# Attention scores as float32 products on two 64-row halves of TensorE, and the softmax by head halves

## What is computed

```
layer 0:  y = layernorm(x) * (1 + gamma1) + beta1
          x = x + attention(y) * tanh(cond @ a1) * 0.1
          z = layernorm(x) * (1 + gamma2) + beta2
          x = x + (gelu(z @ fc1 + b) @ fc2 + b) * tanh(cond @ a2) * 0.1
layer 1:  h = layernorm(x) * (1 + scale) + shift
          q, k = rotary(h @ wq + bq), rotary(h @ wk + bk)
          x = x + softmax(where(mask, q k^T / 4, -inf)) v @ wo + bo
          h = layernorm(x) * (1 + scale) + shift
          x = x + gelu(h @ ff_w1 + b) @ ff_w2 + b
attention: softmax(q k^T / 4) v, per sequence and head, 64 by 64 scores
```

## Time and profile before

| what | value |
|---|---|
| median of 3 runs | 1850.09 us (1849.64 to 1850.42) |
| the profiled execution | 1850.1 us, of which the span of instructions is 1848.3 |
| TensorE matmul busy | 1785.7 us, 97% |
| VectorE busy | 1243.2 us, 67% |
| ScalarE busy | 1229.7 us, 67% |
| GpSimd (POOL) busy | 849.7 us, 46% |
| granted TensorE clock | 0.99 of full on average |
| DMA | 199.84 MB, mean 108 GB/s |
| scores L1077 | 1536 products; mask L1082: 256 |

### The profile page before, as it was taken

How to read it: one execution, slowest core, us unless ns; L and a number is a source line. 1 busy time by engine, 2 the same in 40 slices (tenths; PEclk the granted TensorE clock), 3 DMA queues, 4 the chain that set the end, 5 groups by cost and what they waited for, 6 DMA issues and landing times.

```text
span 1848.3 us, 41687 instructions
## 1 busy us (share of the span) xinstructions
PE 1785.7 (97%) x12623; PEld 1634.5 (88%) x12623; DVE 1243.2 (67%) x2985; ACT 1229.7 (67%) x2265; POOL 849.7 (46%) x1036
## 2 busy tenths in 40 slices
PE   7699999999999999998999999999999999999998
PEld 6688989888989988988889989999999999999986
DVE  6767676667676667676667666776666776666751
ACT  4466766766777766676657766667766667766663
POOL 2233433333433333343635556555566555566544
PEclk8999999999999999999999999999999999999999
DMA  6544435444444435445343333333333333333320
GB/s 165 149 107 126 126 92 123 108 108 127 128 105 105 123 95 133 121 120 120 109 149 104 87 106 93 103 98 108 82 112 93 104 98 108 82 112 92 95 73 34
DMA packets 330275, 199.84 MB, mean 108 GB/s; under 512 B 160994, under 2 KB 314596, under 8 KB 330212
## 3 DMA queue, kind: packets, MB, share of 16 engines
q1 hardware_dynamic: 330212, 199.06, 40.4%
HBM read 80.98 MB, written 17.33 MB: 53 GB/s over the span
## 4 chain that ended last, share of the span: by engine, by line
PE 72%; DVE 11%; issue 7%; ACT 3%; SPq 2%; POOL 2%; DMA 1%; DVEq 0%; POOLq 0%; ACTq 0%
PE C L963 16%; PE D L1154 16%; PE B L963 9%; PE B L1110 8%; PE A L1077 6%; PE B L1096 5%; PE A L963 4%; PE E L963 4%; DVE mx L1429 3%; PE A L1082 1%; DVE o_sb L1453 1%; DVE exps L1435 1%; PE E L1121 1%; PE E L1029 1%; SPq L331 1%
## 5 line engine op out<-in xcount | busy, mean ns | idle before, releaser
L593 POOL TENSOR_TENSOR h_lo<-hact,h_hi 128x512 fp32r<-128x512 f32 x256 | 330.3, 1290 | 251.3 <-ACT h_hi L788 238.5
L1077 PE MATMUL A<-k_pad,q_pad 128*128 128x256 f32 x1536 | 256.7, 294 | 10.3 <-DVE exps L1435 7.1
L1154 PE MATMUL D<-wgt_hi,h_hi 128*128 128x256 f32 x1024 | 263.6, 290 | 0.0
L797 ACT COPY probs_turned<-B 128x512 f32<-128x512 f32 x256 | 149.4, 584 | 169.4 <-PE B L1096 169.2
L1110 PE MATMUL B<-v_blocks,probs_turned 128*128 128x68 f32 x2048 | 254.8, 272 | 1.5 <-ACT probs_turned L797 1.5
L1154 PE MATMUL D<-wgt_lo,h_hi 128*128 128x256 f32 x1024 | 255.7, 282 | 0.0
L1110 PEld LDWEIGHTS B<-v_blocks,probs_turned 128*128 128x128 f32 x2048 | 249.2, 193 | 6.8 <-ACT probs_turned L797 2.6
L783 ACT ACTIVATE hact<-C,b_col 128x512 f32<-128x512 f32 x256 | 175.9, 687 | 83.8 <-PE C L963 81.6
L1077 PEld LDWEIGHTS A<-k_pad,q_pad 128*128 128x128 f32 x1536 | 211.7, 192 | 14.1 <-issue 8.0
L792 ACT ACTIVATE exps<-exps 128x512 f32<-128x512 f32 x256 | 161.4, 632 | 87.4 <-DVE exps L1435 85.3
L1429 DVE TENSOR_REDUCE mx<-A 128x8 f32<-128x512 f32 x256 | 174.2, 681 | 66.1 <-PE A L1082 40.0
(11 more groups left out here) (141 smaller groups left out, 3864.6 us busy)
## 6 DMA issues: line engine op xcount, KB each, us to landing
k_pad<-k_flat SPq DMA_DIRECT2D x512, 64.0 KB, 2.1
q_pad<-q_flat SPq DMA_DIRECT2D x256, 128.0 KB, 2.3
gates<-gates SPq DMA_DIRECT2D x64, 256.0 KB, 4.5
x_bias<-x_bias SPq DMA_DIRECT2D x32, 512.0 KB, 3.5
rotation<-rotation SPq DMA_DIRECT2D x256, 64.0 KB, 1.9
x_in<-in_x SPq DMA_DIRECT2D x16, 512.0 KB, 4.5
gates<-gated_bias SPq DMA_DIRECT2D x32, 256.0 KB, 4.8
x_res<-in_x SPq DMA_DIRECT2D x16, 512.0 KB, 3.9
```

The costliest lines, as they stand in the source:

```text
L593: pool.tensor_tensor(hb[1][:, m % 2, :], hact[:, m % 2, :], hb[0][:, m % 2, :].bitcast(F32), ALU.subtract).then_inc(h_lo, 1)
L1077: ins = nc.tensor.matmul(dst, qpad[g % 2][:, c, p, b, :, :].rearrange("p x s -> p (x s)"), kpad[g % 2][:, c, q, :, b * S:(b + 1) * S], sta ...
L1154: ins = nc.tensor.matmul(Dk[g // 2][:, (g % 2) * D:(g % 2 + 1) * D], hb[p][:, m % 2, g * P:(g + 1) * P], w_slice(q, W_FF2, D, m, 0, D), st ...
```

## The change

Queries and keys stay whole float32 values: q_flat, k_flat, q_pad and k_pad lose the dimension of high and low parts, and `low_qk`, `rotated_low` and the casts of layer 1 fall away. In layer 1 POOL's addition writes the flat buffer itself. `scores` is now called once per group. It makes both sequences' scores as float32 products of 64 rows, 128 weight columns and 128 moving columns: rows 0 to 63 (head half h = 0) into bank A0, rows 64 to 127 (h = 1) into A1, the two halves in turn. In layer 1 two products of 64 rows and 512 columns put the mask row in first, one per bank, with mean_w = 2/128. The second index of all softmax functions is now the head half h instead of the sequence b. The bank of `scores(g)` is free only when `subtract` of both halves of group g-1 is through. TensorE's list: `back(5)` and `hidden(7)` move from the end of a step to behind scores(0) of the next, `back(7)` from behind second_turn(1) to behind scores(1). `scores(3)` moves behind `queries_keys(2)`. ScalarE: `second_norm(3)` now stands ahead of `hidden(7)`, and `second_high(0)` ahead of both exponentials of group 0. VectorE: the first maximum, subtract, maximum, subtract stand together, then z_scale and z_shift. POOL's list is unchanged but for `rotated_low`.

```diff
-        flat = [sb("q_flat", [P, G, KC, 2, P], F32R), sb("k_flat", [P, G, KC, 2, P], F32R)]
-        qpad = [sb(f"q_pad{n}", [P, KC, 2, 2, NX, S], F32R) for n in range(2)]
-        kpad = [sb(f"k_pad{n}", [P, KC, 2, NJ, P], F32R) for n in range(2)]
+        flat = [sb("q_flat", [P, G, KC, P]), sb("k_flat", [P, G, KC, P])]
+        qpad = [sb(f"q_pad{n}", [P, KC, 2, NX, S]) for n in range(2)]
+        kpad = [sb(f"k_pad{n}", [P, KC, 2, P]) for n in range(2)]
...
 # sync
-                    sp.dma_start(kpad[n][r, :, :, j, :].rearrange("p c q n -> p (c q) n").bitcast(F32),
-                                 flat[1][r, g, :, :, :].rearrange("p c q n -> p (c q) n").bitcast(F32))\
-                      .then_inc(spread_in[n], 16)
+                    sp.dma_start(kpad[n][r, :, j % 2, :], flat[1][r, g, :, :]).then_inc(spread_in[n], 16)
...
 # gpsimd, rotated()
-                pool.tensor_tensor(rot_sum[:, i % KC, :], rot_sum[:, i % KC, :], rot_swap[:, i % KC, :], ALU.add)\
-                    .then_inc(rot_added, 1)
+                pool.tensor_tensor(flat[i < KC][:, :, i % KC, :], by_group(rot_sum[:, i % KC, :]),
+                                   by_group(rot_swap[:, i % KC, :]), ALU.add).then_inc(rot_added, 1)
...
 # scalar, step()
+                if c is not None:
+                    second_norm(u - 1, G - 1)
                 if p is not None:
                     hidden(u - 2, p, MC - 1)
                     hidden_high(u - 2, MC - 1)
                 if c is not None:
-                    second_norm(u - 1, G - 1)
+                    second_high(u - 1, 0)
                 if b is not None:
                     exponential(u, 0, 0)
-                if c is not None:
-                    second_high(u - 1, 0)
-                if b is not None:
                     exponential(u, 0, 1)
...
 # tensor
-            def scores(u, layer, g, b, a):
...
+            def scores(u, layer, g, a):
+
+                pe.wait_ge(spread_in[g % 2], upto(u, 2 * NSPREAD, (g // 2 + 1) * NSPREAD))
+                if layer == 1 and g == 0:
+                    pe.wait_ge(mrow_in, upto(u - NT, 16, 16))
+                await_(pe, s_sub, upto(u, 2 * G, 2 * g))
...
+                rows = [slice(64 * h, 64 * h + 64) for h in range(2)]
+                if layer == 1:
+                    for h in range(2):
+                        row = mrow[rows[h], 2 * g * S:2 * (g + 1) * S].rearrange("p (b o s) -> p b o s", b=2, o=1)\
+                            .to_broadcast([64, 2, 4, S])
+                        nc.tensor.matmul(A[h][:, :], mean_w[rows[h], :], row, start=True, stop=False, skip_group_check=True)
+                for b in range(2):
+                    for c in range(KC):
+                        for h in range(2):
+                            n = 2 * b + c
+                            ins = nc.tensor.matmul(A[h][:, n * P:(n + 1) * P],
+                                                   qpad[g % 2][rows[h], c, b, :, :].rearrange("p x s -> p (x s)"),
+                                                   kpad[g % 2][rows[h], c, :, b * S:(b + 1) * S], start=layer == 0,
+                                                   stop=True, skip_group_check=True)
+                            if n == 3:
+                                ins.then_inc(pe_s, 1)
...
 # tensor, step()
                 if b is not None:
-                    scores(u, b, 0, 0, a)
+                    scores(u, b, 0, a)
+                if p is not None:
+                    back(u - 2, MC - 3)
+                    hidden(u - 2, MC - 1)
                 if c is not None:
                     second_turn(u - 1, 0)
-                if b is not None:
-                    scores(u, b, 0, 1, a)
                 if p is not None:
                     back(u - 2, MC - 2)
                 if b is not None:
-                    scores(u, b, 1, 0, a)
+                    scores(u, b, 1, a)
+                if p is not None:
+                    back(u - 2, MC - 1)
+                if b is not None:
                     turn_probs(u, 0, 0, a)
-                    scores(u, b, 1, 1, a)
                     turn_probs(u, 0, 1, a)
...
                 if c is not None:
                     second_turn(u - 1, 1)
-                if p is not None:
-                    back(u - 2, MC - 1)
...
-                    scores(u, b, 3, 0, a)
                 if a is not None:
                     queries_keys(u + 1, a, 2, b)
                 if b is not None:
+                    scores(u, b, 3, a)
                     turn_heads(u, 2, c)
-                    scores(u, b, 3, 1, a)
...
-                if c is not None:
-                    back(u - 1, 5)
-                    hidden(u - 1, 7)
...
 # vector, step()
                     maximum(u, 0, 0)
-                if c is not None:
-                    z_scale(u - 1, 0)
-                if b is not None:
                     subtract(u, 0, 0)
                     maximum(u, 0, 1)
-                if c is not None:
+                    subtract(u, 0, 1)
+                if c is not None:
+                    z_scale(u - 1, 0)
                     z_shift(u - 1, 0)
```

More of the change, by code:

```diff
@@ L679, in step @@
                     hidden_low(u - 1, 4)
-                if a == 1:
-                    rotated_low(u + 1, 2)
-                    rotated_low(u + 1, 3)
                 if n is not None:
@@ L753, in second_high, with lay_flat @@
                 nc.scalar.copy(pair_of(zb[0], pair), E[:, :].rearrange("p (c n) -> p c n", c=KC)).then_inc(z_hi, 1)
-            def high_qk(tile, layer, i):
+            def lay_flat(tile, i):
                 c, keys = i % KC, i < KC
@@ L869, in step @@
                 if a == 0:
-                    high_qk(u + 1, 0, 0)
+                    lay_flat(u + 1, 0)
                 if c is not None:
@@ L877, in step @@
                 if a == 0:
-                    high_qk(u + 1, 0, 1)
+                    lay_flat(u + 1, 1)
                 if b is not None:
@@ L898, in step @@
                 if a == 0:
-                    high_qk(u + 1, 0, 3)
+                    lay_flat(u + 1, 3)
                 if known(u) and u == NT:
@@ L1069, in scores @@
                 if g == 0 and known(u) and u == 0:
-                    pe.wait_ge(*chunk_taken(u, 0, b))
+                    pe.wait_ge(*chunk_taken(u, 0, 1))
                 if g == G - 1 and a is not None:
-                    pe.wait_ge(*chunk_taken(u + 1, a, b))
-                s = slice((2 * g + b) * S, (2 * g + b + 1) * S)
-                for c in range(KC):
-                    dst = A[b][:, c * 256:(c + 1) * 256]
-                    for p, q in BY_WEIGHTS:
-                        ins = nc.tensor.matmul(dst, qpad[g % 2][:, c, p, b, :, :].rearrange("p x s -> p (x s)"),
-                                               kpad[g % 2][:, c, q, :, b * S:(b + 1) * S], start=(p, q) == (0, 0),
-                                               stop=layer == 0 and (p, q) == BY_WEIGHTS[-1])
-                    if layer == 1:
-                        row = mrow[:, s].rearrange("p (o s) -> p o s", o=1).to_broadcast([P, NJ, S])
-                        ins = nc.tensor.matmul(dst, mean_w[:, :], row, start=False, stop=True)
@@ L1086, in turn_probs @@
+            def turn_probs(u, g, h, a):
                 if g == 0:
-                    pe.wait_ge(v_moved, upto(u, 8, 4 * b + 4))
+                    pe.wait_ge(v_moved, upto(u, 8, 4 * h + 4))
                 else:
-                    pe.wait_ge(pv_norm, upto(u, 2 * G, 2 * g + b - 1))
-                if a is not None and g == 2 and b == 1:
+                    pe.wait_ge(pv_norm, upto(u, 2 * G, 2 * g + h - 1))
+                if a is not None and g == 2 and h == 1:
                     pe.wait_ge(y_lo, upto(u + 1, 2, 2))
@@ L1097, in turn_probs, with weigh_values @@
                 ins.then_inc(pe_pt, 1)
-            def weigh_values(u, layer, g, b):
-                if b == 0 and g % 2 == 0:
+            def weigh_values(u, layer, g, h):
+                if h == 0 and g % 2 == 0:
                     pe.wait_ge(v_moved, upto(u, 8, 4 * (g // 2) + 4))
@@ L1624, in step @@
                     subtract(u, 3, 0)
-                if a == 0:
-                    low_qk(u + 1, 2)
                 if a == 1:
@@ L1637, in step @@
                     gate_heads(u, 2)
-                if a == 0:
-                    low_qk(u + 1, 3)
                 if known(u) and u == -1:
```

156 lines of the change are left out of this document (60 added, 96 removed).

## The result

The changed kernel takes **1921.65 us** (1918.64 to 1922.42, median of 4 runs), the kernel before 1850.12 on the same chip (1849.64 to 1850.42, 4 runs): ratio 1.0384, 95% interval 1.0369 to 1.0399. It is 3.8% slower. The forecast was 1914.

The account below looks back on a forecast made before the run. TensorE and VectorE were taken as level in the step's first third, so waits decide. Layer 0 (14 x 2.35 + 2 x 1.1 = 35) and layer 1 (16 x 1.8 = 29) gave +64 on 1850.1: 1914 us, range 1868 to 1975.

Parts of the forecast that it names:

- The price of a block: TensorE's time for one new score block of a group: 1.1 us in layer 0, 1.4 in layer 1.
- (a): From the start of the step (end of project(3)) to second_turn(1): +1.65 us in layer 0, +0.9 in layer 1.
- The exponentials aren't late: ScalarE's exponentials of group 0 were placed as done at about 8.4 and 8.9 us after project(3).
- at the same distance: In layer 1 h_lo(7) was taken to come as long after project(3) as in layer 0, 8.5 us.
- (b): From second_turn(1) to project(0), with VectorE's run deciding: -0.4 us a step in both layers.
- (c): From weigh_values(2,1) to turn_probs(3,0): +1.1 us a step in layer 0, +1.3 in layer 1.
- The sign named for being right: The step is 57.2 us in both layers, TensorE's waits grow to several us, and blocks take 1.1 and 1.4 us.
- The low parts at nothing: Removed low-part work on VectorE, ScalarE, POOL and DMA was priced at nothing, down to -5 us over the kernel.
- Halves one after another: Rival: the two row halves of a score block don't overlap, blocks of 1.8 and 2.25 us, 1969 us; chance 0.2.
- A drain at every change of mode: Rival: TensorE drains at each tiling-mode change, about 0.25 us each, giving 1930 to 1946 us; chance 0.1.
- Faster: Rival: waits are covered and TensorE's work decides, 74 us less, 1776 us; chance 0.12.

Follow-up runs that it names:

- POOL's: The changed kernel with hidden_low(7) ahead of x1_bias in POOL's list: 1912.19 us.
- ScalarE's edit: The changed kernel with exponential(0,0) ahead of second_high(0) in ScalarE's list: 1917.45 us.
- the pair: The changed kernel with hidden_low(7) ahead of x1_bias on POOL and exponential(0,0) ahead of second_high(0) on ScalarE: 1901.11 us.
- back7_late: The changed kernel with back(7) put back behind second_turn(1) in TensorE's list: 1989.61 us.
- three_moves: The changed kernel with scores(3) ahead of queries_keys(2), back(7) behind second_turn(1) and exponential(0,0) ahead of second_high(0): 1852.05 us.
- arithmetic_alone: The new score arithmetic with TensorE's, ScalarE's and VectorE's lists put back in the order of the kernel before: 1902.75 us.
- scores3_first: The changed kernel with scores(3) put back ahead of queries_keys(2) in TensorE's list: 1875.17 us.

## Why the prediction was right

**What bounds the kernel.** Right, and the point on which everything hangs: in the first third of a step TensorE and VectorE are level, so less matmul work gives nothing by itself.

**The price of a block.** Taken as 1.1 and 1.4 us; 1.09 and 1.32 measured (in layer 1 from 1404.64 to the next instruction at 1405.96, 0.33 of it the two mask products). That it fits so closely is partly luck: the instructions start 0.059 us apart and not 0.07, and 0.15 us at the end of the block makes up for it.

**(a)** +1.65 forecast, +1.98 measured in layer 0; +0.9 and +1.03 in layer 1. In layer 0 h_lo(7) came within 0.02 us. "The exponentials aren't late" was wrong: they are 0.8 us later than placed, because second_high(0) waits for z_shift(0), which the working left out. It cost only 0.1 us at turn_probs(0,0) (9.21, placed at 9.1), since h_lo(7) was late in the same place; 0.15 more stands between there and weigh_values(0,0). It did hide what the cure would be: neither POOL's nor ScalarE's edit alone shortens (a) by more than 0.2 us, the pair does by 0.6. In layer 1 the working was wrong and the number right by luck: h_lo(7) isn't "at the same distance" of 8.5 but comes at 8.03, and the last part of back(7) starts at 8.68, placed at 8.65, only because TensorE's own work lasts until then.

**(b)** -0.4 forecast, -0.51 measured in layer 0; -0.4 and -0.68 in layer 1. In layer 0 the two waits, z_lo and ot_lo, stand where they were put, with 0.33 and 0.43 us in the records instead of 1.0 and 0.8. Most of the difference is TensorE's work, put too low: from start to start its pieces take 6.5 us without the two waits, not 5.65 (four transposes 0.44 to 0.6 and not 0.4, hidden(0) 1.6 and not 1.45, and so on). Part of that may be waiting too, since a wait shows in the records only from the modelled end of the one before. It did no harm here, where VectorE decides, but it is why the theories of back7_late, three_moves and arithmetic_alone, which put back(7) into (b), all missed.

**(c)** +1.1 forecast, +1.08 measured in layer 0; +1.3 and +1.17 in layer 1. scores3_first brought (c) to 4.36, below the 4.79 of before, since the block is the cheaper one there.

**The sum.** The sign named for being right, a step of 57.2 us in both layers, came as 57.30 and 57.03. 14 x 2.47 + 2 x 1.1 + 16 x 1.63 = 63 us against the 64 of the forecast. So close a sum is partly luck: layer 0 took 0.12 us a step more than forecast and layer 1 0.17 less. The medians differ by 71.5. The rest lies outside the full steps: the mean granted clock fell from 0.990 to 0.984, which is 30.7 us of full clock missing against 18.5, most of the added 12 in the fill and at the change of layer and the rest in the last 90 us, by the granted clock of the table by stage. The forecast had no term for that. It is why the whole kernel came out 7.65 us above the forecast while the steps came out 1 below.

**The low parts at nothing.** No run tests it alone. DMA fell from 199.84 to 166.30 MB, VectorE's busy time by 30 us and POOL's by about 80, and the only stretches that came out shorter than forecast are (b), by 0.1 us in layer 0 and 0.26 in layer 1, and (c) in layer 1, by 0.14. Whether the low parts have to do with it isn't shown.

**The rivals.** *Halves one after another* fell with 1.64 against 1.09 us per block. *A drain at every change of mode*: TensorE's own rows show 0.09 us between project and the block (602.82 to 602.91), where before no gap stood behind project (580.01), and about 0.15 at its end (16 x 0.059 from 602.91 is 603.85, the next starts at 604.00). So a gap does stand at each change, of about half of the 0.25 taken or less, and the second one is already within the 1.09 of a block; in (c) 0.09 x 32 = 3 us remain and not 16. *Faster* needed h_lo(7) by 7.8 us, which came at 8.48, and VectorE's run in 5.7, which took 6.5 (z_scale(1) at 615.98, low_heads(0) to 622.48).

**What the change did, split.** The arithmetic with the old lists costs 53 us (1902.75 less 1849.3): its block of a whole group needs both halves of the group before subtracted, so less of TensorE's work can lie beside the softmax. The moves add 19: scores(3) behind queries_keys(2) costs 1.5 us a step (4.36 to 5.87), back(7) out of (b) gives 0.9 back (8.15 to 7.29). The clock differs between these two, so the split is good to some 10 us. With a list made for it the same arithmetic is 12 to 13 us faster than the kernel before, of the 74 that the removed TensorE work came to, since VectorE's chain in (b) still takes its time.

## What to carry to other kernels

Where two engines are level, price a change by the chain that ends each stretch: list for every instruction that moves when its last input is ready, on all engines' queues, and check the queue neighbours too, since one overlooked wait (here z_shift in front of the exponentials) moves what comes behind. An arithmetic change that coarsens a block removes places where other work could be put, and the list has to be written anew for it, as a whole: single moves gave 46 us, gave less than 10 or lost 68, eight together turned +71 into -13. Read a small gain step by step: of the 20 us of the pair on POOL and ScalarE the steps hold 8. When taking a wait off one engine, look whether the next engine's chain is the same length, and whether the idle time so made brings the granted clock down.

## What the runs showed of the hardware that was not expected

Float32 products on 64 rows: 16 instructions start 0.059 us apart when they alternate between low and high rows with a bank each ((1.16 - 0.28) / 15), 0.095 when one half follows the other, 0.112 on the full array. So alternating is worth a factor of 1.5 to 1.6 here (1.64 to 1.09 us). The Trainium skill (TensorEngine Tiling (Array Packing), Theoretical Speedup) gives up to twice the rate where one dimension is 64 or less. Against the full array the trace shows 1.9 per instruction, against the same products in turn 1.6. Whether it takes other rows, another bank or both was not tried.

One wait of 2 us, in a stretch where TensorE was busy 1.78 of 4 us, was followed by some 8 us at about half the granted clock, in 11 of the 12 steady steps of layer 0 of back7_late. Its wait in layer 1 is 1.42 us, and there 5 of the 12 steady steps lost the clock and 7 kept it with the same wait. arithmetic_alone, with 1.75 us at once in every step, lost the clock only in five steady steps (mean 0.980), and three_moves, with two waits of about 0.5 us, in none of its steady steps. What exactly separates these cases was not tried.
